# Edge weights of a graph layer in three rounded passes, with the low part made on GpSimd, and one VectorE instruction for the vector messages of two tiles

## What is computed

```
h = edge_feats                                  # 40000 x 8
for W in (W_mlp1, W_mlp2, W_mlp3):              # 8->64, 64->64, 64->64
    h = 1.679 * silu(h @ W / sqrt(rows of W))
w1, w2, w3, w4 = split(h @ W_mlp4 / 8)          # 64 -> 4 x 128, one row for each edge
s0, s1 = x0[sender], x1[sender]                 # 128 scalars, 128 x 3 vectors
p1 = w1 * s0 * y0;        p2 = (w2 * s0)[:, :, None] * y1[:, None, :]
p3 = w3[:, :, None] * s1 * y0;   p4 = w4 * (s1 . y1) / sqrt(3)
node sums = segment_sum of p1, p4, p2, p3 over the receiver, then two linear maps
```

## Time and profile before

| | us |
|---|---|
| median of three runs | 1437.94 (1435.26 to 1441.78) |
| profiled execution, span from first to last instruction | 1589.5 |
| set-up, 0 to 150 | 150 |
| first mixture of experts, 150 to 792 | 642 |
| transition, 792 to 836 | 44 |
| edge loop, 836 to 1450 | 614 |
| rest, 1450 to 1590 | 140 |

### The profile page before, as it was taken

The page is one execution under the profiler, slowest core; times in us unless marked ns, Lnnn a source line. Parts: engine busy times, 40 slices in busy tenths (PEclk is TensorE's granted clock), DMA queues, the critical chain, the costliest instruction groups (busy, mean ns, idle before and its releaser), DMA issues.

```text
span 1589.5 us, 24654 instructions
## 1 busy us (share of the span) xinstructions
PE 1419.4 (89%) x8774; PEld 848.8 (53%) x8774; DVE 1163.6 (73%) x1635; ACT 994.4 (63%) x2000; POOL 916.9 (58%) x762
## 2 busy tenths in 40 slices
PE   5938999998999999999969888888888889888998
PEld 3626748883788568865743333333333333334887
DVE  7887729991899469964966777776778767675655
ACT  6347638881788468855745666776667766664443
POOL 4145658888888888888345555555556555553000
PEclk9868999999999999999999999999999999999999
DMA  9356392768267764654366777776777767765431
GB/s 329 121 208 195 106 382 56 265 212 307 38 249 274 234 209 145 213 174 113 57 212 196 231 222 232 236 231 213 232 232 242 236 209 235 227 205 183 147 107 53
DMA packets 91603, 316.56 MB, mean 199 GB/s; under 512 B 23754, under 2 KB 25988, under 8 KB 80859
## 3 DMA queue, kind: packets, MB, share of 16 engines
q1 hardware_dynamic: 45832, 202.57, 34.1%
q0 software_dynamic: 45648, 112.41, 27.6%
HBM read 378.96 MB, written 77.16 MB: 287 GB/s over the span
## 4 chain that ended last, share of the span: by engine, by line
PE 67%; DVE 20%; issue 6%; ACT 2%; another core or an unknown queue 2%; DMA 2%; DVEq 0%; SPq 0%; POOL 0%; ACTq 0%; POOLq 0%
PE pair L1599 29%; DVE arena L1049 10%; PE pair L1741 9%; PE pair L1636 5%; PE pair L1761 4%; DVE arena L1044 3%; PE pair L1855 3%; PE pair L1866 3%; PE pair L1653 3%; PE pair L1758 2%; PE pair L1590 2%; PE pair L1703 1%; PE pair L1807 1%; ACT arena L1227 1%
## 5 line engine op out<-in xcount | busy, mean ns | idle before, releaser
L1916 POOL DMA_INDIRECT sorted_edges<-arena x311 | 460.7, 1481 | 108.8 <-issue 95.4
L1953 POOL DMA_INDIRECT arena<-node_table,arena x352 | 336.5, 956 | 278.1 <-DVE arena L1049 178.7
L910 DVE TENSOR_TENSOR weights_hl<-arena,weights_hl 128x1024 fp32r<-128x1024 f32 x342 | 405.4, 1223 | 63.4 <-ACT weights_hl L1242 58.6
L1242 ACT ACTIVATE weights_hl<-arena 128x1024 fp32r<-128x1024 f32 x342 | 352.0, 1059 | 47.4 <-PE pair L1599 45.4
L1599 PE MATMUL pair<-weights_hl,rows_hl 128*128 128x512 f32 x1368 | 328.0, 397 | 4.6 <-ACT weights_hl L1242 3.0
L1049 DVE TENSOR_TENSOR arena<-pair,arena 128x768 f32<-128x768 f32 x352 | 318.7, 947 | 0.0
L1599 PEld LDWEIGHTS pair<-weights_hl,rows_hl 128*128 128x128 f32 x1368 | 253.2, 189 | 70.7 <-DVE weights_hl L910 10.2
L1741 PE MATMUL pair<-arena 64*128 64x512 f32 x704 | 216.0, 655 | 57.7 <-DVE arena L1049 45.0
L1044 DVE TENSOR_TENSOR arena<-pair,arena 128x512 f32<-128x512 f32 x176 | 120.4, 684 | 163.8 <-PE pair L1741 113.6
L1403 ACT ACTIVATE arena<-pair 128x512 f32<-128x512 f32 x176 | 105.4, 599 | 109.1 <-remote 88.8
L1761 PE MATMUL pair<-arena 128*32 128x256 f32 x2112 | 154.2, 380 | 21.4 <-issue 16.2
(11 more groups left out here) (292 smaller groups left out, 1550.9 us busy)
## 6 DMA issues: line engine op xcount, KB each, us to landing
arena<-in_w SPq DMA_DIRECT2D x73, 2048.0 KB
arena<-in_w SPq DMA_DIRECT2D x85, 1024.0 KB
sums<-arena SPq DMA_DIRECT2D x88, 512.0 KB
other_down<-in_w SPq DMA_DIRECT2D x8, 1024.0 KB
arena<-in_v SPq DMA_DIRECT2D x16, 512.0 KB, 4.6
pair_rows<-arena SPq DMA_DIRECT2D x1, 5934.0 KB
arena<-pair_rows SPq DMA_DIRECT2D x23, 256.0 KB
arena<-node_table,arena POOLq DMA_INDIRECT x352
```

The lines of the kernel that those rows point to most:

```text
L910: v.tensor_tensor(out=part[s][:, 1], in0=by_chunk(n)[4], in1=part[s][:, 0].bitcast(F32), op=ALU.subtract).then_inc(v_low, 1)
L1242: a.activation(out=part[s][:, 0], in_=cols, func=ACT.Copy).then_inc(a_high, 1)
L1916: g.indirect_dma_start(out=sorted_edges, out_offset=bass.IndirectOffsetOnAxis(ap=slot_i[:, j:j + 1], axis=0), in_=er[:, j, :], in_offset=N ...
L1953: g.indirect_dma_start(out=row, out_offset=None, in_=table, in_offset=bass.IndirectOffsetOnAxis(ap=senders[:, i:i + 1], axis=0)).then_inc( ...
```

## The change

`weights_of` now makes each pair's edge weights in three passes on fp32r parts instead of two fp32 matmuls: twelve 64 x 128 by 64 x 512 matmuls per step instead of four fp32 ones. The high part of the hidden values is a second ScalarE activation of the same PSUM (`h3_hl[r % 2][:, 0]`); the low part is a GpSimd subtraction over 128 x 512 elements, once per batch, which stands in GpSimd's program after the fourth gather of the batch and on which `weights_of` of the batch's first tile waits (`low_h3`). The matrix is split once, ahead of the loop, by one ScalarE copy and one VectorE subtraction. Columns of the matrix are ordered differently for odd tiles, so that w3 and w4 of two tiles lie side by side and one VectorE instruction of 1536 elements per partition makes what two of 768 made; it raises `v_msg` by two at its end. Four semaphores are merged into two, since one more was needed.

```diff
@@ messages_of
-                for t in range(2):
-                    w34 = tp[:, t * 512 + 256:(t + 1) * 512].rearrange("p (w u) -> p w u", w=2)
-                    v.tensor_tensor(out=m[:, t, 2:8].rearrange("p (w m) u -> p w m u", w=2),
-                                    in0=w34.unsqueeze(2).to_broadcast([128, 2, 3, MUL]),
-                                    in1=rows_in[:, t, 1:4].unsqueeze(1).to_broadcast([128, 2, 3, MUL]),
-                                    op=ALU.mult).then_inc(v_msg, 1)
+                w12 = tp[:, :].rearrange("p (q w u) -> p q w u", q=4, w=2)[:, 0:4:3]
+                v.tensor_tensor(out=m[:, :, 0:2], in0=w12, in1=rows_in[:, :, 0:1].to_broadcast([128, 2, 2, MUL]),
+                                op=ALU.mult)
+                w34 = tp[:, 256:768].rearrange("p (w u) -> p w u", w=4)
+                v.tensor_tensor(out=m[:, :, 2:8].rearrange("p t (w m) u -> p t w (m u)", w=2),
+                                in0=w34.unsqueeze(2).to_broadcast([128, 4, 3, MUL]),
+                                in1=rows_in[:, :, 1:4].rearrange("p t m u -> p t (m u)").unsqueeze(2).to_broadcast(
+                                    [128, 2, 2, 3 * MUL]),
+                                op=ALU.mult).then_inc(v_msg, 2)
@@ mlp_function, layer 3
+                    if r >= 2:
+                        a.wait_ge(low_h3, r - 1)
+                    a.activation(out=h3_hl[r % 2][:, 0].rearrange("p (h x) -> p h x", h=2), in_=b, func=ACT.Silu,
+                                 scale=SILU_2MOM / 8)
                     a.activation(out=act3[r % 2].rearrange("p (h x) -> p h x", h=2), in_=b, func=ACT.Silu,
                                  scale=SILU_2MOM / 8).then_inc(a_mlp, 1)
@@ ahead of the loop, VectorE and ScalarE
+            v.wait_ge(a_high, ALONE * NCH + 1)
+            v.tensor_tensor(out=m4_hl[:, 1], in0=m4_sb, in1=m4_hl[:, 0].bitcast(F32),
+                            op=ALU.subtract).then_inc(v_low, 1)
...
+            a.activation(out=m4_hl[:, 0], in_=m4_sb, func=ACT.Copy).then_inc(a_high, 1)
@@ weights_of
                 if i % BT == 0:
-                    pe.wait_ge(a_mlp, mlp_place[batch, 3] + 1)
+                    pe.wait_ge(low_h3, batch + 1)
+                if i == 0:
+                    pe.wait_ge(v_low, ALONE * NCH + 1)
                 if i >= Q:
                     pe.wait_ge(v_msg, i - Q + 2)
-                for h in range(2):
-                    p = slice(64 * h, 64 * (h + 1))
-                    mm = pe.matmul(out=tp_bank[(i + h) % Q], lhsT=act3[batch % 2][p, k * 128:(k + 1) * 128], rhs=m4_sb[p],
-                                   start=True, stop=True)
+                for a, b in PASSES:
+                    for h in range(2):
+                        p = slice(64 * h, 64 * (h + 1))
+                        mm = pe.matmul(out=tp_bank[(i + h) % Q], lhsT=h3_hl[batch % 2][p, a, k * 128:(k + 1) * 128],
+                                       rhs=m4_hl[p, b], start=a + b == 0, stop=a == 1, skip_group_check=True)
                 mm.then_inc(p_tp, 1)
@@ GpSimd
+            def low_hidden_of(r):
+
+                g.wait_ge(a_mlp, mlp_place[r, 3] + 1)
+                g.tensor_tensor(out=h3_hl[r % 2][:, 1], in0=act3[r % 2], in1=h3_hl[r % 2][:, 0].bitcast(F32),
+                                op=ALU.subtract).then_inc(low_h3, 1)
+
...
             for i in range(NTILE):
                 gather(i)
+                if i % BT == Q - 1:
+                    low_hidden_of(i // BT)
```

More of the change, by code:

```diff
@@ L306, in program @@
         other_down = [w.rearrange("p (k d) -> p k d", k=4) for w in (other_down0, other_down1, other_spare)]
+        h3_0, h3_1, m4_hl = phase_tensors(edge_hidden_hl0=(1024, F32R), edge_hidden_hl1=(1024, F32R),
+                                          edge_weights_hl=(1024, F32R))
+        h3_hl = [h.rearrange("p (s c) -> p s c", s=2) for h in (h3_0, h3_1)]
+        m4_hl = m4_hl.rearrange("p (s c) -> p s c", s=2)
         acc = dram("node_sums", [N + TILE, D])
@@ L376, in program @@
         x_blank, fill_set, small_set = sem("x_blank"), sem("fill_set"), sem("small_set")
-        v_insub, v_key, v_hit, v_leaf, v_ids, v_eps, v_norm = (sem(n) for n in (
-            "in_sub_made", "limits_made", "limits_passed", "leaf_found", "ids_known", "eps_added", "normed"))
+        v_search, v_hit, v_leaf, v_ids, v_eps, v_norm = (sem(n) for n in (
+            "search_inputs_made", "limits_passed", "leaf_found", "ids_known", "eps_added", "normed"))
         v_scale, v_bounds, v_member, v_across, v_xseg, v_rowtot, v_starts, v_slots = (sem(n) for n in (
@@ L388, in program @@
         p_turn, p_logit, p_before = sem("turned_up"), sem("logits"), sem("counted_before")
-        v_picked, v_pairs, v_tiles, v_gap, v_route = (sem(n) for n in (
-            "picked", "pairs_known", "tiles_known", "gap_known", "routed"))
+        v_picked, v_pairs, v_tiles, v_route = (sem(n) for n in (
+            "picked", "pairs_known", "tiles_known", "gap_and_weights_known"))
         a_high, v_low, p_part = sem("weights_high"), sem("weights_low"), sem("weights_used")
@@ L399, in program @@
         a_pick, a_mlp = sem("last_picks_made"), sem("mlp_activated")
+        low_h3 = sem("edge_hidden_low")
         a_sum, a_kept = sem("sums_copied"), sem("sums_kept")
@@ L665, in vector @@
             T.did(v.scalar_tensor_tensor(out=in_sub, in0=K["node"], scalar=hi_p, in1=lowq,
-                                         op0=ALU.is_lt, op1=ALU.mult), v_insub, 1)
+                                         op0=ALU.is_lt, op1=ALU.mult), v_search, 1)
             v.wait_ge(a_mids, 2)
@@ L688, in vector @@
             T.did(v.tensor_tensor_scan(out=limit, data0=least, data1=least, initial=2 * BIG, op0=ALU.min,
-                                       op1=ALU.min), v_key, 1)
+                                       op1=ALU.min), v_search, 2)
             def tree_ids(b, n):
@@ L797, in vector @@
                     T.wait()
-                    T.did(v.tensor_tensor(out=gap2, in0=top2, in1=top1, op=ALU.subtract), v_gap, 1)
+                    T.did(v.tensor_tensor(out=gap2, in0=top2, in1=top1, op=ALU.subtract), v_route, 1)
                 T.wait()
@@ L821, in vector @@
             T.wait()
-            T.did(v.tensor_tensor(out=wt[1], in0=wt[0], in1=gap2, op=ALU.mult), v_route, 1)
+            T.did(v.tensor_tensor(out=wt[1], in0=wt[0], in1=gap2, op=ALU.mult), v_route, 2)
             v.wait_ge(p_before, 1)
@@ L1043, in messages_of @@
                 v.wait_ge(p_tp, first // 2 + 1)
-                v.tensor_tensor(out=m[:, :, 0:2],
-                                in0=tp[:, :].rearrange("p (t w u) -> p t w u", t=2, w=4)[:, :, 0:2],
-                                in1=rows_in[:, :, 0:1].to_broadcast([128, 2, 2, MUL]), op=ALU.mult)
-                for t in range(2):
-                    w34 = tp[:, t * 512 + 256:(t + 1) * 512].rearrange("p (w u) -> p w u", w=2)
-                    v.tensor_tensor(out=m[:, t, 2:8].rearrange("p (w m) u -> p w m u", w=2),
-                                    in0=w34.unsqueeze(2).to_broadcast([128, 2, 3, MUL]),
-                                    in1=rows_in[:, t, 1:4].unsqueeze(1).to_broadcast([128, 2, 3, MUL]),
-                                    op=ALU.mult).then_inc(v_msg, 1)
+                w12 = tp[:, :].rearrange("p (q w u) -> p q w u", q=4, w=2)[:, 0:4:3]
[7 more added lines that the diff above has]
+                                op=ALU.mult).then_inc(v_msg, 2)
             v.wait_ge(p_up, NT)
@@ L1218, in scalar @@
             copy_turned(NT - 1)
-            a.wait_ge(v_gap, 1)
+            a.wait_ge(v_route, 1)
             a.activation(out=gap2, in_=gap2, func=ACT.Exp).then_inc(a_exp, 1)
@@ L1355, in apply_node @@
                              bias=shift[:, t:t + 1]).then_inc(a_norm, 1)
+            a.wait_ge(p_part, begun[FT])
+            a.wait_ge(d_late, 64)
+            a.activation(out=m4_hl[:, 0], in_=m4_sb, func=ACT.Copy).then_inc(a_high, 1)
             root(NORMS[0])
@@ L1473, in spin @@
                     pe.matmul(out=bank[:, :], lhsT=ident, rhs=K["node"][:, 0:512], start=True, stop=True)
-            pe.wait_ge(v_insub, 1)
+            pe.wait_ge(v_search, 1)
             for t in range(NT):
@@ L1479, in tensor @@
             mm.then_inc(p_first, 1)
-            pe.wait_ge(v_key, 1)
+            pe.wait_ge(v_search, 2)
             def id_rows_of(tiles):
@@ L1899, in gpsimd @@
             g.wait_ge(g_rec, 5)
-            g.wait_ge(v_route, 1)
+            g.wait_ge(v_route, 2)
             g.wait_ge(v_pairs, 2)
@@ L2200 @@
         w_mlp23=np.tile(np.concatenate([g["W_mlp2"], g["W_mlp3"]], 1), (2, 1)),
-        w_mlp4=np.tile(g["W_mlp4"].reshape(HID, 4, MUL)[:, [1, 0, 2, 3]].reshape(HID, 4 * MUL), (2, 1)),
+        w_mlp4=np.concatenate([g["W_mlp4"].reshape(HID, 4, MUL)[:, o].reshape(HID, 4 * MUL)
+                               for o in ([1, 0, 2, 3], [2, 3, 1, 0])], 0),
```

## The result

The changed kernel takes 1469.41 us (median of four runs, 1467.58 to 1470.45) against 1438.68 for the kernel before: a ratio of 1.0211, 95% interval 1.0179 to 1.0243, or 30.7 us more. The forecast was 1458 and slower.

A forecast was written before the change was run, and what follows sets the result against it. Unprofiled, TensorE was taken to bound the edge loop at 5.41 us per step (476 us); GpSimd at 5.64 would replace it (496 us), so 1437.9 + 20 = 1458 us, with an 8-in-10 range of 1408 to 1490.

The forecast's parts named there:

- What sets the unprofiled loop: Edge loop before: TensorE binds at 5.41 us per step, 476 us in all, VectorE and GpSimd close behind.
- The place of the difference: The 151.6 us between profiled span and median were placed in the edge loop, as TensorE stalls mostly absent from unprofiled runs.
- a loop of 590 to 625 us and a span near 1590: Profiled execution of the changed kernel: TensorE's stalls were expected to persist and leave GpSimd idle.
- TensorE's part: Edge weights: three fp32r passes, halves side by side, 0.87 us per pair; step from 5.41 to 5.03 us.
- Rival 3: Edge weights: fp32r halves run one after the other, TensorE at 6.39 us per step, 1524 us in all; chance 0.05.
- VectorE's part: Messages: one instruction of 1536 elements takes 1.66 us instead of 1.73, saving 0.14 per step; floor 5.01.
- GpSimd's part: Gathers and low part: subtraction of 1.2 us per batch, two steps 11.28 us, 5.64 per step.
- The sum: Edge loop: GpSimd at 5.64 replaces TensorE at 5.41, 496 us against 476, 20 us more, 1458 us.
- Rival 1: Edge loop: GpSimd is not the bound, gather gaps being the profiler's; 27 us less, 1411 us; chance 0.28.
- Rival 2: Edge loop: even, if before was at 5.57 per step or the subtraction costs 0.65; 1433 to 1444 us; chance 0.17.
- The merged count of messages: Messages: `v_msg` rises for both tiles at the end, delaying a gather 0.87 us, hidden by eight buffers.
- The latency of the new wait: Edge loop: cycle from one low part to the next is 9.4 us against 11.28, so throughput decides.

The follow-up runs named there:

- e1: The kernel before, unchanged, traced again on the first chip: 1440.2 us, with a span of 1438.2 us.
- e5: The changed kernel with messages in two VectorE instructions as before, on a chip where the kernel before takes 1596.46 us: 1602.69 us, ratio 1.0031.
- e9: e2 with half the bytes per gather, on a chip where the kernel before takes 1596.46 us: 1621.57 us, ratio 1.0140.
- e12: The kernel of e9 again, on a chip where the kernel before takes 1635.14 us: 1645.10 us, ratio 1.0067.
- e13: The kernel of e5 again, on a chip where the kernel before takes 1635.14 us: 1604.58 us, ratio 0.9856 to before.
- e4: The kernel before with only the merged message instruction and its column order: 1436.30 us, ratio 0.9979.
- e11: The changed kernel with the low-part subtraction on VectorE instead of GpSimd, on the first chip: 1447.07 us, ratio 1.0060 to before.
- e2: The changed kernel without GpSimd's subtraction, the third pass using the high part again: 1432.25 us, ratio 0.9950 to before.
- e10: The changed kernel with the subtraction after the second gather of a batch instead of the fourth, on the first chip: 1482.75 us, ratio 1.0295 to before.

## Why the prediction was right, point by point

**What sets the unprofiled loop.** The conclusion held: TensorE at 5.335 us per step (5.41 taken), busy 99% (e1). The place of the difference was read rightly too: of the 151.3 us between the spans 1589.5 and 1438.2, 144.5 lie between the first and the last message of the loop (611.3 against 466.8). The reason given for it did not hold: the prediction put the stalls of the earlier trace rows down to the recording. e1 was recorded too and has none, and on other chips all runs of the kernel before take about 1596 and 1635 us. That the times came from an unstalled chip was luck; on the chips of e5 to e9 and of e12 and e13 a forecast of 20 us more would have had no ground. One forecast that hung on this reason missed: a loop of 590 to 625 us and a span near 1590 for the profiled execution of the changed kernel. They are 494 to 497 and 1465.8 us.

**TensorE's part.** Side by side, as taken; 0.755 us per pair instead of 0.87, since the 0.18 us for filling and the switch come to 0.07. This error had no effect on the sum, as TensorE left the bound either way. Rival 3 is out. The rule of the Trainium skill that was cited there (TensorEngine Tiling (Array Packing), Key Properties) agrees with the trace for fp32r on 64 rows too: six matmuls, each recorded with 0.39 us, in 0.755.

**VectorE's part.** 1.67 us against 1.66. What e4 gained, 3.4 us, is what a saving behind the bound gives.

**GpSimd's part.** A subtraction is 1.28 us long and adds 1.15 per batch, since the gap behind it is 0.16 and not 0.30 us; 1.2 was taken, from copies counted twice and a rounding that no row showed, so that it came this near is partly luck. Two steps were forecast at 11.28 us and a batch in the middle of the loop took 11.21. The mean was 11.30 (2 x 5.650), because GpSimd waits once at the start of the loop, 4.26 us for the first messages (gather at 844.95); the forecast had no such term, and its 0.07 us too much per batch nearly made up for it. The Trainium skill (GPSIMD Engine Reference, Elementwise — side-by-side cycle accounting) gives an estimate of 1.11 us for 512 elements before the fixed part; the trace agrees, with 1.28 in all. Its advice to make such an operation on VectorE is borne out in direction, as the subtraction takes 0.68 us there and e11 is 22 us faster than the changed kernel.

**The sum.** The loop after was forecast at 496 us; it is 494.4 from the first to the last message start and 496.7 with the last pair. The loop before was put at 476 and is 469.1 by the same count. So the term that was mis-sized is the loop before, 7 us too long: the middle of 462 and 490 was taken, where TensorE's floor of 471 stood beside it. That is most of the gap between 20 us forecast and 30.7 measured; the rest, 3 us, lies between single spans and medians.

**The rivals.** Rival 1 asked whether the 0.30 us between gathers vanish without recording. The comparison of spans and medians above says that they don't: 352 gathers at 1.25 us and 44 subtractions set the changed kernel's time, 1465.8 us recorded and 1469.4 in the median. Its price was wrong too: without GpSimd's extra work the loop takes 5.22 us per step and not 5.1 (e2), a gain of 7.5 us and not 27. Most of the missing 20 us is that the loop before was shorter than the 5.41 taken (7 us) and that e2 is at 5.22 and not 5.1 (some 10), with four engines at 96 to 97%. The prediction's floor of 5.04 for GpSimd was in the text, but the sum of rival 1 supposed cheaper gathers. Rival 2 is out as well: the loop before was not at 5.57, and the subtraction does not cost 0.65.

**The merged count of messages** cost nothing that e4 could show. **The latency of the new wait** (9.4 us of 11.28) was judged right: from 850 us on GpSimd waits for nobody in the changed kernel, and with the wait gone e10 is not faster. What the prediction had not seen is that the place decides which VectorE instruction the subtraction meets.

## What to carry to other kernels

An engine that looks half idle in a profile may be idle because of stalls elsewhere: count its cadence per loop step (here 4 x 1.26 = 5.04 us of 5.34) before giving it work, and compare the profiled span with the timed runs, as a trace from a stalled execution hides the bound of an unstalled one. Per-instruction floors of all engines, put side by side, foretold the new loop within 1%, with some luck; the old loop was the harder number. Where several engines are within a few per cent of each other, as in e2, taking work off one of them brings less than the floors promise. In this loop, work on GpSimd also had to be placed against VectorE's instructions with two inputs in SBUF.

## What was not expected of the hardware

- VectorE's 128 x 256 multiplication of two SBUF tensors takes 0.41 us alone and 2.03 us when GpSimd's 1.28 us subtraction of two SBUF tensors falls into it (e10). It is held until 0.29 us after the subtraction's end, while the subtraction keeps its 1.28 to 1.29 us. The recorded starts leave a question open: in some cases the subtraction starts 0.46 us or more after the multiplication, which by itself would have been over. Message instructions, with one input in PSUM, kept their 1.74 to 1.75 us, also in the 41 cases in which a subtraction of the changed kernel overlaps one of 1536 elements. The Trainium skill (GPSIMD Engine Reference, Key points) says that GpSimd shares its SBUF interfaces with VectorE and names VectorE instructions with two SBUF inputs; the trace agrees, and adds that the VectorE instruction waited for longer than the whole subtraction.
- A GpSimd subtraction with the same tensor as both inputs takes 1.05 us, with two tensors 1.28.
- The same program takes 1439, 1596 or 1635 us on three chips. In the trace of the kernel before with a span of 1589.5 us the difference lies in the edge loop and goes with stalls of TensorE for which the trace names no releaser; for 1635 us there is no trace of the kernel before.
